# A three-stage decoder kernel: the causal mask of self attention as extra stack rows and four small column tiles, and the parts of the row maxima on GpSimd in place of VectorE

## The reference, cut to what matters

```python
q, k, v = split(x @ Wqkv.T + bqkv)           # 16 heads of 16
q, k = rope(q), rope(k)
att = einsum('bhqd,bhkd->bhqk', q, k) * scale
att = where(causal, att, -inf)               # key <= query
y = einsum('bhqk,bhkd->bhqd', softmax(att), v)
x = layernorm(x + y @ Wo.T + bo)
```

## Time and profile before

| | us |
|---|---|
| median of three runs | 1184.74 |
| lowest and highest | 1183.73, 1185.34 |
| the profiled execution, its own time | 1184.21 |
| its span | 1182.4 |

### The profile page before, as it was taken

One profiled execution on the slowest core, in us unless ns is written; L12 is line 12 of the kernel. 1 busy time (PEld: TensorE's weight loads), 2 busy tenths in 40 slices (PEclk: granted clock), 3 DMA queues, 4 the chain that ended last, 5 costly groups with the idle time before them and its releaser, 6 DMA issues.

```text
span 1182.4 us, 30629 instructions
## 1 busy us (share of the span) xinstructions
PE 1113.7 (94%) x11732; PEld 920.0 (78%) x11732; DVE 954.8 (81%) x2219; ACT 669.1 (57%) x1703; POOL 661.2 (56%) x714
## 2 busy tenths in 40 slices
PE   6899999799999999888999999999999999999997
PEld 5667666566666766556899899999999899988887
DVE  6768877887878878867788888888888888868977
ACT  5466564577777777564555444444444444558663
POOL 4467564645555555264778554444544455737665
PEclk9899999999999999989999999999999999999999
DMA  5875544354444444302111000000000100101111
GB/s 160 212 185 132 128 125 112 97 138 123 126 121 131 119 126 126 104 21 89 61 66 55 1 1 1 1 1 1 1 1 1 37 2 1 37 19 36 37 37 36
DMA packets 107491, 83.05 MB, mean 70 GB/s; under 512 B 74172, under 2 KB 95804, under 8 KB 107346
## 3 DMA queue, kind: packets, MB, share of 16 engines
q1 hardware_dynamic: 107345, 81.10, 24.6%
HBM read 57.02 MB, written 23.07 MB: 68 GB/s over the span
## 4 chain that ended last, share of the span: by engine, by line
PE 56%; DVE 14%; issue 6%; POOL 4%; ACT 2%; SPq 1%; DMA 0%; POOLq 0%; DVEq 0%; ACTq 0%
PE bank L1632 5%; PE bank L1633 5%; PE bank L1634 5%; PE bank L1688 4%; PE bank L1661 4%; PE bank L663 4%; PE bank L641 3%; PE bank L560 3%; DVE B_nr L803 2%; PE bank L1648 2%; PE bank L1703 2%; PE bank L1701 2%; PE bank L1702 2%; PE bank L1649 2%; PE bank L1650 2%
## 5 line engine op out<-in xcount | busy, mean ns | idle before, releaser
L1936 POOL TENSOR_TENSOR C_QK<-C_t1b,C_t2b 128x512 f32<-128x512 f32 x128 | 168.8, 1319 | 227.2 <-DVE C_t2b L1775 226.6
L1772 DVE SCALAR_TENSOR_TENSOR C_t1b<-bank,C_bcol,C_tabs 64x512 f32<-64x512 f32 x256 | 192.0, 750 | 38.4 <-PE bank L1634 34.3
L803 DVE TENSOR_REDUCE B_nr<-bank 128x4 f32<-128x512 f32 x256 | 164.3, 684 | 24.3 <-PE bank L602 23.8
L1062 ACT ACTIVATE PT<-bank 128x512 f32<-128x512 f32 x224 | 130.1, 596 | 92.4 <-PE bank L641 90.8
L1632 PE MATMUL bank<-C_XTh,C_Wh 128*128 128x512 f32 x256 | 112.4, 439 | 5.7 <-DVE C_XTl L1621 1.9
L1868 ACT ACTIVATE C_P<-bank,C_nm 128x128 f32<-128x128 f32 x256 | 90.7, 367 | 34.2 <-DVE C_nm L1785 32.6
L1887 ACT ACTIVATE C_V<-bank 128x512 f32<-128x512 f32 x64 | 38.1, 597 | 124.1 <-PE bank L1650 122.5
L1633 PE MATMUL bank<-C_XTl,C_Wh 128*128 128x512 f32 x256 | 101.7, 397 | 0.0
L1634 PE MATMUL bank<-C_XTh,C_Wl 128*128 128x512 f32 x256 | 101.2, 395 | 0.0
L663 PE MATMUL bank<-PT,vpool 128*32 128x128 f32 x2048 | 97.1, 285 | 2.0 <-ACT OTf L1072 2.0
L1775 DVE SCALAR_TENSOR_TENSOR C_t2b<-bank,C_bcol,C_tabs 128x512 f32<-128x512 f32 x128 | 96.1, 751 | 1.8
(11 more groups left out here) (271 smaller groups left out, 3495.8 us busy)
## 6 DMA issues: line engine op xcount, KB each, us to landing
Adrq<-PB SPq DMA_DIRECT2D x16, 192.0 KB, 3.0
Adrk<-PB SPq DMA_DIRECT2D x16, 192.0 KB, 3.2
stk<-Adrq SPq DMA_DIRECT2D x16, 192.0 KB
stk<-Adrk SPq DMA_DIRECT2D x16, 192.0 KB
Bdrq<-PB SPq DMA_DIRECT2D x16, 192.0 KB, 3.0
stk<-Bdrq SPq DMA_DIRECT2D x32, 96.0 KB
Bdrk<-PB SPq DMA_DIRECT2D x16, 192.0 KB, 2.8
stk<-Bdrk SPq DMA_DIRECT2D x32, 96.0 KB
```

Of the source, the lines that this page charges most:

```text
L803: e.tensor_reduce(dst, bank[n % 2][:, :].rearrange("p (a b) -> p a b", a=4), AX.X, ALU.max, negate=True).then_inc(sem("m_dve"), 1)
L1062: e.activation(pt_of(n)[:, :], bank2(n)[:, :], ACT.Exp).then_inc(sem("e_act"), 1)
L1772: e.scalar_tensor_tensor(out=v4(t1b[kq][lo:lo + 64, :]), in0=v4(o[hi:hi + 64, :]), scalar=bc[hi:hi + 64, :], in1=tabsC[hi:hi + 64, 2 * kq ...
L1936: e.tensor_tensor(QK[v % 3][:, kq, :], t1b[kq][:, :], t2b[kq][:, :], ALU.add).then_inc(sem("rc_pool"), 1)
```

## The change

- The stacks of stage A get three more rows. On the query side rows 96 to 98 are a one-hot of the query's block of 32 positions (blocks 0, 1, 2), on the key side row r holds -1e30 where the key's block is above r. Their product masks all blocks of 32 by 32 above the diagonal. The maxima's parts move to rows 99 to 101. `pass1` now takes 99 rows, `pass2` 102, and both 512-column mask matmuls are gone.
- The four diagonal blocks get their mask from `causal_blocks`: four matmuls, each of 32 weight columns (a column tile) and 128 moving columns, into the finished bank. `causal1` does it for `pass1`'s bank and now raises `s_pe`; `causal2` for `pass2`'s and raises `t_pe`. Both stand behind `pass1` and `pass2` and ahead of `pv`.
- `shift_parts` of stage A moves from DVE to POOL, behind `rope_sum` in its step, as in stage B.
- The constant rows are loaded before the loop by two DMAs in place of one (3 rows for the queries, 6 for the keys, of 10 buffers).

```diff
-        e.tensor_copy(nmb[L][:, :, :, 0, :], heads(nr)).then_inc(sem(name), 1)
+        e.tensor_copy(nmb[L][:, :, :, 0, :], heads(nr)).then_inc(sem("sh_pool"), 1)
...
-                if not L:
-                    q.wait_ge("consts", 1)
-                    q.wait_ge("ld_m", 48)
-                    e.matmul(scores, causalTb[:, :], identb[:, :].unsqueeze(1).to_broadcast([128, 4, 128]),
-                             start=True, stop=False, skip_group_check=True)
...
-                    rows, h = (slice(64 * t, 64 * t + 48), hs[j] % 16) if L else (slice(0, 96), hs[j])
+                    rows, h = (slice(64 * t, 64 * t + 48), hs[j] % 16) if L else (slice(0, 99), hs[j])
...
-            q.wait_ge(*(("sh_pool", 4 * g - 60) if L else ("sh_dve", 4 * g + 4)))
+            q.wait_ge("sh_pool", 4 * g + 4)
...
-                if not L:
-                    q.wait_ge("consts", 1)
-                    e.matmul(bank2(n)[:, :].rearrange("p (a b) -> p a b", a=4), identb[:, :],
-                             causalTb[:, :].unsqueeze(1).to_broadcast([128, 4, 128]), start=True, stop=False, skip_group_check=True)
...
-                    rows, h = (slice(64 * t, 64 * t + 54), hs[j] % 16) if L else (slice(0, 99), hs[j])
+                    rows, h = (slice(64 * t, 64 * t + 54), hs[j] % 16) if L else (slice(0, 102), hs[j])
...
+        def causal_blocks(o, left, right, name):
+
+            for g in range(4):
+                own = slice(32 * g, 32 * g + 32)
+                m = e.matmul(o[own, :].rearrange("p (a b) -> p a b", a=4)[:, :, own], left[:, own],
+                             right[:, own].unsqueeze(1).to_broadcast([128, 4, 32]), start=False, stop=True, skip_group_check=True)
+            m.then_inc(sem(name), 1)
+
+        def causal1(n):
+            q.wait_ge("consts", 1)
+            q.wait_ge("ld_m", 48)
+            causal_blocks(bank[n % 2], causalTb, identb, "s_pe")
+
+        def causal2(n):
+            causal_blocks(bank2(n), identb, causalTb, "t_pe")
...
+            for n in pass1_units(s):
+                if n < NA:
+                    causal1(n)
+            for n in pass2_units(s):
+                if n < NA:
+                    causal2(n)
+            if s < NA:
                 for n in pv_units(s):
                     pv(n)
...
-            if s in shifts and shifts[s] < 16:
-                shift_parts(e, q, shifts[s], "sh_dve")
...
-            if s in shifts and shifts[s] >= 16:
-                shift_parts(e, q, shifts[s], "sh_pool")
+            if s in shifts:
+                shift_parts(e, q, shifts[s])
...
-                row = 64 * hg + 48 if L else 96
+                row = 64 * hg + 48 if L else 99
...
-            load(STK[96:99, :, :].rearrange("p (i s) x -> p i s x", s=32)[:, :, 16:32, :],
-                 ot[0:3, :].rearrange("p (s x) -> p s x", x=128).unsqueeze(1).to_broadcast([3, 10, 16, 128]), "ones_A")
+            for half, rows in enumerate((3, 6)):
+                load(STK[96:96 + rows, :, :].rearrange("p (i s) x -> p i s x", s=32)[:, :, 16 * half:16 * half + 16, :],
+                     edge[3 * half:3 * half + rows, :].rearrange("p (s x) -> p s x", x=128).unsqueeze(1).to_broadcast([rows, 10, 16, 128]),
+                     "ones_A")
```

More of the change, by code:

```diff
@@ L132, in program @@
     tabs_ready = ("ld_A", 32), ("ld_B", 48)
-    ot = I["c_one"]
+    ot, edge = I["c_one"], I["c_edge"]
     NA, NN = 64, 320
@@ L462, in split, with shift_parts @@
             e.tensor_tensor(pb[:, 2, :, :], y_[:, :, :], pb[:, 1, :, :], ALU.subtract).then_inc(sem(sp(kp, 0)[0]), 1)
-    def shift_parts(e, q, g, name):
-        L, b = divmod(g, 16)
+    def shift_parts(e, q, g):
+        L = g // 16
         q.wait_ge("m_dve", last_unit(g, NK[L] - 1) + 1)
@@ L471, in shift_parts @@
         heads = lambda a: a[:, :, :].rearrange("p k (g h) -> p g k h", h=16)
-        e.tensor_copy(nmb[L][:, :, :, 0, :], heads(nr)).then_inc(sem(name), 1)
[L473 to L478, removed]
+        e.tensor_copy(nmb[L][:, :, :, 0, :], heads(nr)).then_inc(sem("sh_pool"), 1)
+        q.wait_ge("sh_pool", 4 * g + 1)
+        e.tensor_tensor(heads(nb[L]), heads(nr), nmb[L][:, :, :, 0, :], ALU.subtract).then_inc(sem("sh_pool"), 1)
+        q.wait_ge("sh_pool", 4 * g + 2)
+        e.tensor_copy(nmb[L][:, :, :, 1, :], heads(nb[L])).then_inc(sem("sh_pool"), 1)
+        q.wait_ge("sh_pool", 4 * g + 3)
+        e.tensor_tensor(nmb[L][:, :, :, 2, :], heads(nb[L]), nmb[L][:, :, :, 1, :], ALU.subtract).then_inc(sem("sh_pool"), 1)
     def pe_ab(e, steps):
@@ L585, in pass1 @@
                     if not L:
-                        q.wait_ge("ones_A", 16)
+                        q.wait_ge("ones_A", 32)
                 if n % U[L] == 0 or (L and n % 8 == 0):
@@ L600, in pass1 @@
                     i3 = b % len(QS[L])
-                    rows, h = (slice(64 * t, 64 * t + 48), hs[j] % 16) if L else (slice(0, 96), hs[j])
+                    rows, h = (slice(64 * t, 64 * t + 48), hs[j] % 16) if L else (slice(0, 99), hs[j])
+                    alone = bool(kd) if L else j == 0
                     m = e.matmul(bank[n % 2][:, j * 128:j * 128 + 128], QS[L][i3][rows, h, :], (AS if kd else KS[L])[i3][rows, h, :],
-                                 start=bool(kd), stop=bool(kd) or j == 3, skip_group_check=not kd)
-                    if j == 3:
+                                 start=alone, stop=bool(kd) or bool(L and j == 3), skip_group_check=not kd)
+                    if L and j == 3:
                         m.then_inc(sem("s_pe"), 1)
@@ L638, in pass2 @@
                     i3 = b % len(QS[L])
-                    rows, h = (slice(64 * t, 64 * t + 54), hs[j] % 16) if L else (slice(0, 99), hs[j])
+                    rows, h = (slice(64 * t, 64 * t + 54), hs[j] % 16) if L else (slice(0, 102), hs[j])
                     alone = bool(L) and (adds_mask(n) or not is_masked(n))
                     m = e.matmul(bank2(n)[:, j * 128:j * 128 + 128], (AS if kd else KS[L])[i3][rows, h, :], QS[L][i3][rows, h, :],
-                                 start=alone, stop=alone or j == 3, skip_group_check=not alone)
-                    if j == 3:
+                                 start=alone or not (L or j), stop=alone or bool(L and j == 3), skip_group_check=not alone)
+                    if L and j == 3:
                         m.then_inc(sem("t_pe"), 1)
+        def causal_blocks(o, left, right, name):
[10 more added lines that the diff above has]
+            causal_blocks(bank2(n), identb, causalTb, "t_pe")
         def pv(n):
@@ L2430, in tables @@
     c["c_one"][3:6] = 0
+    block = np.arange(2048) % 128 // 32
+    r = np.arange(3)[:, None]
+    c["c_edge"] = np.concatenate([block == r, np.where(block > r, f(-1e30), f(0)), np.ones((3, 2048))]).astype(f).astype(bf)
     c["c_pick"] = np.repeat(np.eye(32, dtype=f), 3, axis=0).astype(bf)
```

2 lines of the change are left out of this document (1 added, 1 removed).

## The result

| | us |
|---|---|
| kernel before, median of the runs beside it | 1184.24 (1181.42 to 1186.41) |
| changed kernel, median | 1189.82 (1186.84 to 1192.63) |
| ratio | 1.0051, 95% interval 1.003 to 1.0072 |
| the profiled execution of the changed kernel, its own time | 1190.13 |
| its span | 1188.3 |

A second set of runs of the changed kernel gave 1188.22 beside 1184.11, ratio 1.0038 (1.0025 to 1.005). So the change costs 4 to 6 us, where a gain of 5.4 was forecast. Times are medians of a set; a profile shows one execution, which can lie some us beside that median. In the profile after, L598 is `pass1`, L633 `pass2`, L642 `causal_blocks`, L671 `pv`, L609 the turn of the maxima's parts (L613 of before), L818 the maxima on VectorE, L681 and L691 the turning of outputs, L1004 and L1007 ScalarE's split, L985 and L987 its evacuation `ab`; GpSimd's lines have their old numbers.

The account below looks back on a forecast made before the run. In stage A, SP's queue was taken to bound up to 59.4 us and from 158 to 195, PE between. Steps 16 to 19 -0.9, nine groups -4.3, late `pass2` -0.2: -5.4 from 1184.7, hence 1179.3 us; range 1171 to 1187.5.

Parts of the forecast that it names:

- Masks, 0.32 us a unit: On PE, two mask matmuls of 0.43 us give way to two tile sets of 0.11: 0.32 us saved a step.
- The parts on GpSimd, 0.8 us: Four small operations behind L449 on POOL were taken to last 0.8 us, within 0.65 to 1.5.
- The rule of the Trainium skill: Keep elementwise work on VectorE, GpSimd being 1.96 times slower; by it the four operations take about 1.3 us on POOL.
- The cosine's 0.98 us: POOL's L449 waits 0.98 us for `rope_cos` on DVE; with the parts gone from DVE that wait goes.
- The race: PE against POOL at the turn: PE there after 6.2 us, POOL's parts after 6.9; a group takes 9.47, not 9.95.
- The rival "slower": POOL's chain becomes the bound, turn beyond 7.5 us behind PE's start: +4.8 in nine groups, 1188.4 us; chance 0.14.
- The start at 0: One DMA more, 0.32 us on SP between 14.62 and 20.17 where its queue is idle, costs 0.
- SP's stretch from 158 us: From 158 to 195 us SP's queue sets the time, so the change gives 0, at best -2.6 us.
- PE keeps what it saves: Rival: POOL is in time at the turn, each group wins 4 x 0.32 us, 11.5 over nine, 1172 us; chance 0.20.

Follow-up runs that it names:

- parts_first: The changed kernel with GpSimd making the maxima's parts ahead of the split and rope in its step: 1182.27 us, ratio 0.999 to before.
- heavy_load: The kernel before with only the larger constant load, its added rows never read: 1185.44 us beside 1183.99, ratio 1.0013.
- masks_only: The changed kernel with stage A's parts of the maxima back on VectorE: 1187.56 us beside 1184.11, ratio 1.0025.
- cos_ahead: `masks_only` with constants loaded early and rope's cosine ahead of the parts on VectorE: 1189.1 us, ratio 1.0038 to before.
- first_early: The changed kernel with the parts ahead of GpSimd's rope chain and buffers 1 to 9's constants loaded early: 1178.83 us, ratio 0.9951; repeat 1180.06, ratio 0.9966.
- split_later: `first_early` with ScalarE's first half of the split moved behind the next step's shift and evacuation: 1178.4 us beside 1183.96, ratio 0.9947.

## Why the prediction was wrong, step by step

- **Masks, 0.32 us a unit: right.** 0.33 measured, two sets in 0.13 us. PE reaches the turn at 6.31 in `parts_first`, where 6.2 was said.
- **The parts on GpSimd, 0.8 us: a little short.** From 109.22 to the end at 110.28 they take 1.06 us: each operation about 0.2, and 0.28 from start to start. The rule of the Trainium skill (GPSIMD Engine Reference, Performance versus the Vector engine) that I set against the move had given an estimate of 1.3, as far off on the other side. Its ratio of 1.96 doesn't hold at this size: the cast takes 0.20 us at the median on GpSimd and 0.16 at the least on VectorE, the subtraction 0.22 and, in the trace of before, 0.17.
- **The cosine's 0.98 us: the step that failed.** The wait goes, but the prediction took it as 0.98 us off GpSimd's chain. The cosine now falls into the time of L462 and L438, and there the two engines take turns: the cosine waits for L462 and the first L438 for the cosine, the pair of L438 grows from 1.43 to 1.92 us, and 0.49 is left. L449 ends 6.60 us behind the group's start in the group shown, where 7.14 - 0.98 - 0.1 = 6.06 was counted. It was in sight: the prediction itself said that VectorE's small operations are slow where GpSimd works beside them, and did not apply it to the cosine when moving it beside L462 and L438. The same rows show the turns: the cast of 1.01 us begins at 100.92, 0.17 behind L462, and ends with it.
- **The race.** 6.60 + 1.0 + 0.05 = 7.65 where 6.9 was forecast, 7.66 as the mean of nine groups (6.99). (The means of before are 7.13 and 2.82, not 7.15 and 2.80; the sum is the same.) Behind the turn 2.44, as forecast (2.48). 9 x (0.67 - 0.04) = 5.7 us more than the 85.2 forecast: 90.9 were measured, and a gain of 4.3 became a loss of 1.4. Of the 0.74 us by which GpSimd missed 6.9, the cosine is 0.54 and the parts' own time 0.2. The rival "slower" named this mechanism and 7.5 us as its point; the turn lies just beyond it. Its price of 1188.4 lies beside what was measured, though by another sum: of its 4.8 us in the nine groups 1.4 came, and the rest came from the ends.
- **The start at 0: wrong.** "Where the queue is idle" was true of SP's queue and not of what stands behind it. In before all 30 packets of the constant load had started when the first stores were issued at 20.17; in `heavy_load` 26 of its 90 start behind the issue at 19.35. `heavy_load` gives it 1.5 us in the median; the two executions of the changed kernel reach step 20 late by 2.2 and 1.6.
- **SP's stretch from 158 us.** The changed kernel lost 4 us more at the end of stage A in its first profiled execution. From 199 to 209 us PE ran at 1.2 GHz:

```profile
196.00:199.00 3.00, 0.94 (x15) 0.50 (x14) 1.35 (x5) 1.31 (x4) 2.13 (x3) 1.00 0.46 143
199.00:209.00 10.00, 9.78 (x89) 6.67 (x88) 4.09 (x9) 3.40 (x6) 3.03 (x9) 0.50 0.39 102
```

  Before it fell, PE had been busy 0.94 of 3 us. In the second execution of the same kernel it was busy 2.60 of those 3 us, the clock stayed at 2.4 GHz, and the 4 us didn't appear. The clock fell there in three of the seven executions that came to the end of stage A later than before did (this one, `masks_only`, `cos_ahead`), all with tiles; the other four have at most 3.4 us of 1.2 GHz between 190 and 240 us. What decides it was not tried and stays open, and so does whether the low clock or what came before it cost the 4 us.
- **PE keeps what it saves: false beyond the turn as well.** Even with the turn free, 2.9 us of the nine groups' 11.5 are won (83.7 against 86.6).

The forecast's first part treated VectorE's parts as the thing to be rid of. The runs say that the gain to be had, 4 to 6 us with both repairs (`first_early`, the fastest version that was tried together with `split_later`), comes for the most part from moving them to GpSimd and ahead of its rope chain. Behind the chain they cost 6 us more with tiles (1188.2 against 1182.3) and 9 with dense masks (1190.3 against 1180.9, in two sets).

## What to carry to other kernels

When an operation is moved to an engine that is already part of a chain, its place in that engine's step is worth more than its duration: put it where its input is ready and ahead of the long operations, and compare both places. A wait that disappears brings two operations together that had been kept apart, and their durations from the old trace hold only for the old overlap. A load into a queue that looks idle is paid for by the next transfers, so read when it lands, and issue it where nothing follows.

## What the runs showed of the hardware

- VectorE's product of 128x512 and GpSimd's products take turns; they don't both run slower. GpSimd's of 128x256 takes 0.71 to 0.79 us; issued while VectorE's is running it takes 1.17 to 1.27 and ends 0.58 to 0.60 behind it. VectorE's takes 0.68 undisturbed; begun while GpSimd's L462 or L438 is running it takes up to 1.59 and ends 0.54 to 0.57 behind it, in 85 of 86 cases (steps 20 to 56 of all sixteen profiles, as above). VectorE's maxima, which read a bank, are not touched: 0.67 to 0.69 us in all 307 cases beside one of GpSimd's long operations. So a small operation pays for what runs on the other engine: the same cast has 198 ns as its median on GpSimd, where it stands behind L449, and 1006 on VectorE, where it meets L462.

```profile
L472 POOL CAST A_nmb<-A_nr x16: 191/198/259, 41.5 to 179.8; 128x16 bf16<-128x16 f32 x16
L474 POOL TENSOR_TENSOR A_nb<-A_nr,A_nmb x16: 218/219/614, 41.8 to 180.1; 128x16 f32<-128x16 f32 x16
```

- Four column tiles of 32 with 128 moving columns each take 0.06 to 0.07 us together, as much as one full matmul of 128 columns; a change from full weights to tiles costs 0.09 us and the change back 0.11.
- Sixty more packets of 4 KB onto 3 to 6 partitions, issued 6 us ahead (`heavy_load`), made two stores of 192 KB land in 5.2 us instead of 2.6.
